# Expert stage of a two-layer kernel: row loads issued by ScalarE instead of SyncE, two tile operations moved from ScalarE to VectorE

## The reference

```
routing_indices = jnp.argmax(einsum(x, router_w), axis=-1)
for e in range(8):
    mask = (routing_indices == e)[..., None]
    xe = jnp.where(mask, x, 0.0)
    g, u = xe @ gate_w[e].T, xe @ up_w[e].T          # 128 -> 352
    out = out + jnp.where(mask, (silu(g) * u) @ down_w[e].T, 0.0)
x = layernorm(x + out)
```

## Time and profile before

| | us |
|---|---|
| median of 3 runs | 936.82 (936.54 to 937.92) |
| profiled execution, its own time | 937.77 |
| span of the profiled execution | 936.0 |
| PE / PEld busy | 680.2 / 492.8 |
| DVE busy | 605.9 |
| ACT busy | 421.8 |
| POOL busy | 684.7 |
| L403 matmuls (gate and up), 852 | 114.5 |
| L413 matmuls (down), 426 | 59.8 |
| L489 scatters, 71 | 73.2 |
| L444 / L439 / L455 on ACT, 71 each | 34.4 / 19.7 / 27.8 |

### The profile page before, as it was taken

The page is one execution under the profiler, slowest core; times in us unless marked ns, Lnnn a source line. Parts: engine busy times, 40 slices in busy tenths (PEclk is TensorE's granted clock), DMA queues, the critical chain, the costliest instruction groups (busy, mean ns, idle before and its releaser), DMA issues.

```text
span 936.0 us, 13364 instructions
## 1 busy us (share of the span) xinstructions
PE 680.2 (73%) x3329; PEld 492.8 (53%) x3329; DVE 605.9 (65%) x1386; ACT 421.8 (45%) x1287; POOL 684.7 (73%) x866
## 2 busy tenths in 40 slices
PE   4657799988898998998989655230720888888884
PEld 1324456665565565665556444120610787777773
DVE  2069999999999999999999998820042132222221
ACT  3554357466566555655655430110120355555553
POOL 0588899999999999999999983877222165555555
PEclk9888989999999999999999787565755799999997
DMA  3532433424334234334342210211163455555551
GB/s 96 133 104 49 117 78 87 119 71 110 96 82 124 72 91 117 81 93 104 82 103 69 68 35 6 79 45 51 35 194 110 144 172 185 177 186 171 186 185 47
DMA packets 145006, 97.27 MB, mean 104 GB/s; under 512 B 95630, under 2 KB 128401, under 8 KB 144802
## 3 DMA queue, kind: packets, MB, share of 16 engines
q1 hardware_dynamic: 139602, 87.66, 33.1%
q0 software_dynamic: 4320, 8.43, 2.9%
q10 hardware_dynamic: 1008, 0.31, 0.1%
HBM read 39.80 MB, written 31.43 MB: 76 GB/s over the span
## 4 chain that ended last, share of the span: by engine, by line
PE 44%; DVE 23%; POOL 17%; issue 9%; ACT 3%; DMA 1%; SPq 1%; POOLq 0%; DVEq 0%; ACTq 0%
PE banks L403 11%; PE banks L704 8%; POOL x_sorted L310 6%; PE banks L413 5%; PE banks L617 4%; POOL q_prod L880 4%; DVE upd L1119 4%; DVE banks L1129 4%; DVE banks L1105 3%; PE banks L672 3%; DVE prod L1090 3%; PE banks L604 3%; DVE banks L1115 3%; DVE mix L1109 3%; DVE upd L1101 2%
## 5 line engine op out<-in xcount | busy, mean ns | idle before, releaser
L617 PE MATMUL banks<-q_prod,ident 128*128 128x256 f32 x512 | 123.3, 396 | 63.1 <-POOL q_prod L880 63.1
L880 POOL TENSOR_TENSOR q_prod<-s_keep,q_gam 128x512 f32<-128x512 f32 x128 | 140.5, 1104 | 33.6 <-ACT s_keep L747 25.1
L617 PEld LDWEIGHTS banks<-q_prod,ident 128*128 128x128 f32 x512 | 99.2, 199 | 89.5 <-POOL q_prod L880 75.1
L525 DVE TENSOR_TENSOR hid<-banks,silu 128x384 f32<-128x384 f32 x71 | 39.6, 558 | 155.8 <-PE banks L413 119.0
L403 PE MATMUL banks<-xs_t,w_tile 128*128 128x128 f32 x852 | 114.5, 286 | 27.0 <-issue 14.7
L747 ACT ACTIVATE s_keep<-banks 128x128 f32<-128x128 f32 x128 | 49.6, 388 | 186.4 <-DVE upd L1119 179.7
L403 PEld LDWEIGHTS banks<-xs_t,w_tile 128*128 128x128 f32 x852 | 104.4, 198 | 38.6 <-issue 23.0
L1129 DVE TENSOR_REDUCE banks<-upd 128x128 f32<-128x640 f32 x128 | 106.0, 828 | 22.3 <-ACT x_ct L856 10.4
L704 PE MATMUL banks<-kkqk,ident 128*128 128x320 f32 x256 | 94.3, 535 | 34.0 <-ACT y_rms L818 20.4
L489 POOL DMA_INDIRECT out<-rows_out,xs x71 | 73.2, 1031 | 40.7 <-ACT rows_out L455 37.6
L1105 DVE TENSOR_REDUCE banks<-prod 128x64 f32<-128x576 f32 x128 | 93.7, 732 | 0.0
(11 more groups left out here) (167 smaller groups left out, 1445.9 us busy)
## 6 DMA issues: line engine op xcount, KB each, us to landing
w_tile<-gate_up_we SPq DMA_DIRECT2D x71, 352.0 KB
xs<-x_sorted SPq DMA_DIRECT2D x71, 64.5 KB
x_ct<-in_x_ct SPq DMA_DIRECT2D x16, 256.0 KB, 3.0
x_sorted<-beta SPq DMA_DIRECT2D x16, 256.0 KB, 2.6
x_sorted<-v_s SPq DMA_DIRECT2D x16, 256.0 KB, 2.6
b_h<-x_sorted SPq DMA_DIRECT2D x16, 256.0 KB, 3.2
v_h<-x_sorted SPq DMA_DIRECT2D x16, 256.0 KB, 3.5
q_dram<-kq_s SPq DMA_DIRECT2D x16, 256.0 KB, 4.0
```

What stands on the lines that cost most here:

```text
L617: i = mm(out, ident[:, :], q_prod[m][:, :, d, :], start=(m == 0 and d == 0), stop=(d == DH - 1), skip_group_check=True)
L880: b.step(label, win, lambda: tt(out, x, y, op))
```

## The change

Three things change, all inside the functions above:

- The loads of the rows (`rows`) leave SyncE's list. They go to ScalarE's: 8 of them ahead of its loop, and then `rows(t+8)` between `variance(t-1)` and `silu_of(t+2)`, with the same `value_load` and the same wait for the scatter of tile t - 4. ScalarE now waits for the routing tables and the padding rows first. SyncE keeps only `weights`, and no longer waits for the padding rows.
- `x_copy` goes from ScalarE to VectorE (a `tensor_copy`), 3 ahead of the loop and then as the first operation of each turn.
- `norm` goes from ScalarE to VectorE (a `tensor_scalar` multiply), behind `row_sum` and ahead of `hidden`.

The orders for each t are then ACT: `variance(t-1)`, `rows(t+8)`, `silu_of(t+2)`; DVE: `x_copy(t+3)`, `row_sum(t-1)`, `norm(t-3)`, `hidden(t+2)`. TensorE's and GpSimd's lists stay as they are.

```diff
@@ -361,21 +361,8 @@
                               gate_up_we[:, :, :, :].rearrange("p e g i -> p (e g i)")[:, bass.ds(at, 2 * I)]
                               .rearrange("p (g i) -> p g i", g=2)).then_inc(s_w[tile % NG], 16)
 
-            def rows(tile):
-                row = eng.value_load(row_at[0:1, tile:tile + 1], min_val=0, max_val=E * REGION + (E - 1) * P)
-                after_dma(eng, s_scat, tile - NR)
-                eng.dma_start(xs[tile % NR][:, :], t["x_sorted"][bass.ds(row, P), :]).then_inc(s_xs[tile % NR], 16)
-
-            eng.wait_ge(s_pad, 16 * (1 + E))
-            for tile in range(NR - 4):
-                rows(tile)
-                if tile < NG - 1:
-                    weights(tile)
             for tile in range(NF):
-                if tile + NR - 4 < NF:
-                    rows(tile + NR - 4)
-                if tile + NG - 1 < NF:
-                    weights(tile + NG - 1)
+                weights(tile)
             for n in range(NR):
                 eng.wait_ge(s_scat[n], 16 * len(range(n, NF, NR)))
 
@@ -433,11 +420,6 @@
             A = nc.scalar.activation
             nc.scalar.preload_act_table_set("silu_and_others")
 
-            def x_copy(tile):
-                after(eng, s_xturn, tile)
-                after(eng, s_up, tile - NX)
-                A(xs_t[tile % NX][:, :], turn_ps[tile % 2][:, 0:P], ACT.Copy).then_inc(s_xt, 1)
-
             def silu_of(tile):
                 after(eng, s_gate, tile)
                 after(eng, s_hid, tile - 2)
@@ -449,25 +431,24 @@
                 A(res2_sq[tile % 2][:, :], res2[tile % NV][:, :], ACT.Square, scale=D ** -0.5,
                   accum_out=var2[:, tile:tile + 1]).then_inc(s_var, 1)
 
-            def norm(tile):
-                after(eng, s_rstd, tile)
+            def rows(tile):
+                row = eng.value_load(row_at[0:1, tile:tile + 1], min_val=0, max_val=E * REGION + (E - 1) * P)
                 after_dma(eng, s_scat, tile - NR)
-                A(rows_out[tile % NR][:, :], res2[tile % NV][:, 0:D], ACT.Copy, scale=rstd2[:, tile:tile + 1]) \
-                    .then_inc(s_norm, 1)
-
-            for tile in range(3):
-                x_copy(tile)
+                eng.dma_start(xs[tile % NR][:, :], t["x_sorted"][bass.ds(row, P), :]).then_inc(s_xs[tile % NR], 16)
+
+            eng.wait_ge(s_route, n_route_all)
+            eng.wait_ge(s_pad, 16 * (1 + E))
+            for tile in range(NR - 4):
+                rows(tile)
             for tile in range(2):
                 silu_of(tile)
-            for tile in range(NF + 3):
-                if tile + 3 < NF:
-                    x_copy(tile + 3)
-                if 1 <= tile < NF + 1:
+            for tile in range(NF + 1):
+                if 1 <= tile:
                     variance(tile - 1)
+                if tile + NR - 4 < NF:
+                    rows(tile + NR - 4)
                 if tile + 2 < NF:
                     silu_of(tile + 2)
-                if 3 <= tile:
-                    norm(tile - 3)
 
 
         def finish_pool(eng):
@@ -531,11 +512,28 @@
                 v.tensor_tensor(res2[tile % NV][:, 0:D], down_ps[tile % 2][:, 0:D], xs[tile % NR][:, 0:D], ALU.add) \
                     .then_inc(s_sum, 1)
 
+            def x_copy(tile):
+                after(eng, s_xturn, tile)
+                after(eng, s_up, tile - NX)
+                v.tensor_copy(xs_t[tile % NX][:, :], turn_ps[tile % 2][:, 0:P]).then_inc(s_xt, 1)
+
+            def norm(tile):
+                after(eng, s_rstd, tile)
+                after_dma(eng, s_scat, tile - NR)
+                v.tensor_scalar(rows_out[tile % NR][:, :], res2[tile % NV][:, 0:D], rstd2[:, tile:tile + 1], None, ALU.mult) \
+                    .then_inc(s_norm, 1)
+
+            for tile in range(3):
+                x_copy(tile)
             for tile in range(2):
                 hidden(tile)
-            for tile in range(NF + 1):
-                if 1 <= tile:
+            for tile in range(NF + 3):
+                if tile + 3 < NF:
+                    x_copy(tile + 3)
+                if 1 <= tile < NF + 1:
                     row_sum(tile - 1)
+                if 3 <= tile:
+                    norm(tile - 3)
                 if tile + 2 < NF:
                     hidden(tile + 2)
 
```

## The result

The changed kernel takes 956.5 us (median of 4 runs, 955.84 to 959.65) against 937.4 for the kernel before (4 runs, 936.54 to 938.4): the ratio is 1.021, with a 95% interval of 1.0185 to 1.0236. It is slower, as forecast, but by 19 us and not by 5, and its time lies outside the forecast's range of 929 to 953.

A forecast was written before the change was run, and what follows sets the result against it. SyncE's issue time was taken to bound the old kernel; afterwards Loop B would. Start 0, middle +7.9 and end -2.4 gave +5.5 us, 943.3 for the profiled execution, median 942; 8-in-10 range 929 to 953.

The forecast's parts named there:

- SyncE's issue time bounds the kernel before: In the old expert stage, SyncE's row load and weight copy issues set 2.71 us a tile, not transfers.
- x_copy and norm cost nothing: Off ScalarE worth nothing; on VectorE x_copy delays what follows by 0.20 us, norm costs nothing.
- Loop A: One turn, row_sum(t-1)'s end to row_sum(t)'s end, through variance, row load, silu, hidden and x_copy: 2.70 us.
- 1.18 for the row load: Row load on ScalarE between variance and silu, sized as on SyncE: 1.09 to 1.18 us.
- 1.18 + 0.27 + 0.41: Upper bound in us for the row load on ScalarE: long register load, begun behind the accumulator read.
- the register load is slower on ScalarE: Rival, chance 0.22: register load of 0.54, a start behind the accumulator read, or both; 946, 952 or 966 us.
- Its other form: Case of the slower register load rival: ScalarE's load begins only behind the accumulator read; turn 3.08 us, time 952.
- Loop B: Two turns, through variance, rstd, scatter(t-4)'s landing, the row load's wait and silu: 5.77 us, 2.89 a turn.
- the end: Six silus behind the last row load: 12.9 us against 15.3, change -2.4.
- The middle: 52 turns of 2.89 + 0.02 us: 151.3 against 143.4, change +7.9.
- The start: Up to silu(12): 760.9 against 761.0 us, change 0, with silu(0) at 728.0 and TensorE restarting at half clock.
- The floor of a register load: Trainium skill's floor of about 600 ns for a register load from memory; by it Loop A 3.03, time 949 us.

The follow-up runs named there:

- 1: Changed kernel with only the row loads put back on SyncE, x_copy and norm staying on VectorE: 938.0 us, ratio 0.998.
- 3: Changed kernel with the register load ahead of variance and 16 row buffers, so row loads wait for scatter(t-8): 895.1 us, ratio 0.954.
- 7: Changed kernel with the register load ahead of variance and rows 6 tiles ahead instead of 8, 12 buffers: 894.4 us, ratio 0.952.
- 8: As 3, but with x_copy and norm back on ScalarE: 901.0 us, ratio 0.959.
- 4: Changed kernel with weights copied for the first 6 tiles only, the other 65 copies left out: 944.2 us, ratio 1.005.
- 2: Changed kernel with the row's register load moved ahead of variance, wait and DMA issue left behind it: 949.3 us, ratio 1.010.
- 6: Changed kernel with rows(t+8) behind silu(t+2) instead of ahead of it: 920.3 us, ratio 0.981.
- 9: Changed kernel copying only the gate half (176 KB) of each weight copy from tile 6 on: 957.4 us, ratio 1.017.

## Why the prediction was right and where it was wrong

- *SyncE's issue time bounds the kernel before*: shown. With the row loads back on SyncE the pace is 2.73 (1); with them off SyncE and out of loops A and B it is TensorE's floor (3, 7, 8). The rule of the Trainium skill ("DMA: Bandwidth & Descriptors", "Issuing engines are not separate DMA queues") that another queue saves only the sequencer's time is true here, but that time was not small: it was worth 0.64 us of 2.76 a tile, 43 to 45 us in all (3, 7).
- *x_copy and norm cost nothing*: right in the middle (1, 8). The copy took 0.28, with 0.20 until the next operation, the scaling 0.28.
- *Loop A*: its path was right, with every link but one within 0.05 us. The step that failed is the size of one term, "1.18 for the row load", in which the register load stood at SyncE's 0.27. That load took 0.71 in the median and 0.78 in the turn shown, so variance to silu took 1.63. A was 3.12 in the median and not 2.70, and so A decided and not B. In 4, with a load of 0.28, the shortest turns are 2.65. The prediction's own bound for this cost, 1.18 + 0.27 + 0.41, held 1.63, but the forecast and its range didn't use it.
- *The rival "the register load is slower on ScalarE"* (chance 0.22; 946, 952 or 966) is what happened, but longer than its 0.54. Its other form did not: the load didn't wait for the accumulator read: it began with variance, at 827.9, before that read. Nor is the cause a property of ScalarE, as TensorE's load grew too. The hint was in the rows: SyncE's second load took 0.54 where its first took 0.27, and the window at 830.50 above has a weight copy running there. The prediction took the 0.54 as a size and didn't ask for its cause.
- *Loop B*: 5.77 us for two turns was forecast, and 5.78 is the median in 2. What was missed is the tail of the landings (a mean of 6.03 for two turns in 2) and that a landing isn't always 2.4 us (2.9 in 6). Without the long register load B does decide, and the time is 944.2 (4) against 942. Its parts agree too, within 2 us each: silu(12) at 761.9 (760.9 was summed), 153.0 for the middle (151.3) and 11.2 for the end (12.9).
- *The direction* was right by its own mechanism: with the load short, 4 is still slower than the kernel before (1.003 to 1.007), though by 5 us of the 19 only.
- *The middle* came out at +19.8 and not +7.9: 52 x (3.12 - 2.89) = 12 us are the register load. The start was 2.7 us later and not level, the end gave 4.1 and not 2.4. In the start the prediction had TensorE restart at half the clock behind a stop; the granted clock was 0.50 until 729 us and 1.00 from 730 on, so that part of its sum didn't happen, and silu(0) came at 730.4 and not at 728.0. The two errors partly cancel.
- *The floor of a register load.* The Trainium skill gives about 600 ns ("DMA: Bandwidth & Descriptors", "Latency and other measured facts"). Here it was 0.27 to 0.30 us with the DMA engines free, below that floor, and 0.7 to 0.8 beside a copy, above it. The measurement decides. By that page the prediction had 949, nearer to 956.5 than its own 942, but as the load follows the copies and no fixed floor, that is luck.
- *The range* ended at 953. It held two of the rival's three cases and not the third, 966; 956.5 lies between the last two.

## What to carry to other kernels

Moving a DMA issue to an engine that also computes puts its register load, its wait and its issue in front of whatever stands behind it there; add them to every loop of waits that runs through that place, loops over two turns too, before counting the gain on the old queue. Put the register load where the engine waits anyway, and let the issue wait for something several turns old: here the same move went from 2% slower to 5% faster by those two edits. A duration read from one place of the timeline holds for that place: ask what the DMA engines do there and will do in the new one.

## What the runs showed of the hardware

- A register load from on-chip memory (TENSOR_LOAD) took 0.27 to 0.30 us with the DMA engines idle and mostly 0.5 to 0.9 while a 352 KB copy filled them: 0.54 on SyncE in the kernel before, 0.71 on ScalarE and 0.80 on TensorE in the changed one. With half the bytes the median on ScalarE was 0.37, with none 0.28. That the copies cause it is shown (4); by which path is not.
- What counts is where in the copy the load begins, and not how busy the DMA engines are on average. A copy's packets span 1.1 us. Over the ten kernels with whole copies, by the traces' DMA packets, the median load was 0.79 us when it began within 0.1 us of the copy's first packet, 0.58 at 0.2 to 0.4 behind it, 0.54 at 0.4 to 0.6, 0.34 at 0.6 to 0.8 and 0.28 from 0.8 on. So 7 has short loads, although its DMA engines are busier: ScalarE's began 1.04 us behind the copy's first packet there, and 0.07 behind it in the changed kernel.
- A register load runs beside an ACTIVATE in flight: in the turn shown it began with variance, and in 4 it took 0.28 us in that place.
- The scatter's landing was 2.4 us in the median before, in the changed kernel and in 2, 2.7 in 9 and 2.9 in 6, with single ones of 3.3 to 4.7. What makes it longer is open: 4, almost without weight copies, has 2.3 and a longest of 3.4, and 9, with half the bytes, has the longest of all.
- Late landings are late in one part of 16. In 2, a scatter that started at 851.96 had 15 of the 16 updates of its semaphore by 854.37 and the last at 855.44. Over the twelve kernels 79 of 93 such late last updates came within 4 us behind the start of a packet of 16 KB that the trace calls "instruction" and that took 1 us or so; these stretches cover 27% of the time. That the two belong together is suggested by this and tested by no run.
